# Reordering an attention loop: the third batch's output projection between the last two turns of maxima, and four small products at the loop's start

## The reference

```python
x = x + attention(layernorm(x))     # 16 heads of 16, softmax, with biases
x = x + ffn(layernorm(x))           # silu(x W1) * (x W3), Walsh-Hadamard, W2
x = x + memory(layernorm(x))        # gated values, decaying sum along the sequence, gate, Wo
x = x + ffn(layernorm(x))
# attention, for each head:
scores = Q @ K.T / sqrt(16);  attn = softmax(scores);  out = attn @ V
return concat(out) @ Wo.T + bo
```

## Time and profile before

| | |
|---|---|
| three runs | 562.08, 563.42 (median), 564.31 us |
| the profiled execution | 561.39 us, of which 559.6 us is the span from the first to the last instruction |
| TensorE busy in the records | 547.4 us |
| VectorE, ScalarE, GpSimd busy | 385.8, 311.7, 192.6 us |
| the attention loop | from about 34.9 to 242.7 us of the span |

### The profile page before, as it was taken

One profiled execution on the slowest core, in us unless ns is written; L12 is line 12 of the kernel. 1 busy time (PEld: TensorE's weight loads), 2 busy tenths in 40 slices (PEclk: granted clock), 3 DMA queues, 4 the chain that ended last, 5 costly groups with the idle time before them and its releaser, 6 DMA issues.

```text
span 559.6 us, 8472 instructions
## 1 busy us (share of the span) xinstructions
PE 547.4 (98%) x2932; PEld 368.2 (66%) x2932; DVE 385.8 (69%) x727; ACT 311.7 (56%) x581; POOL 192.6 (34%) x221
## 2 busy tenths in 40 slices
PE   8999999999999998999999999999999999999997
PEld 5553343344435433468888888888888888888887
DVE  6898988898898899836475555756886437364433
ACT  3668889876987787753333233366775323323231
POOL 4795367562546252520122012422332012102120
PEclk9999999999999999999999999999999999999999
DMA  7465440230023030021122221210000202223121
GB/s 218 109 197 168 141 134 3 72 127 32 3 97 132 2 152 4 2 75 21 19 43 33 34 42 18 43 18 1 0 2 0 34 12 43 64 39 76 25 52 39
DMA packets 74554, 32.54 MB, mean 58 GB/s; under 512 B 59608, under 2 KB 67800, under 8 KB 74128
## 3 DMA queue, kind: packets, MB, share of 16 engines
q1 hardware_dynamic: 73292, 30.93, 20.6%
q10 hardware_dynamic: 1220, 1.07, 0.6%
HBM read 10.89 MB, written 5.24 MB: 29 GB/s over the span
## 4 chain that ended last, share of the span: by engine, by line
PE 87%; DVE 5%; ACT 3%; issue 2%; SPq 2%; DMA 1%; ACTq 0%; POOL 0%; DVEq 0%
PE PS L426 85%; DVE mxr L1141 2%; SPq L384 2%; PE PS L437 1%; ACT PR L966 1%; DMA xf<-PR 1%; PE PS L624 1%; DMA ring<-mT 1%; ACT AOh L838 0%; DVE PR L1280 0%; DVE OT L1206 0%; ACT PR L1034 0%; ACT XNs L1028 0%; ACTq L928 0%; DVE X L1315 0%
## 5 line engine op out<-in xcount | busy, mean ns | idle before, releaser
L426 PE MATMUL PS<-xTh,ring 128*128 128x512 f32 x608 | 187.5, 391 | 0.0
L1141 DVE TENSOR_REDUCE mxr<-PS 128x1 f32<-128x512 f32 x256 | 162.9, 681 | 24.0 <-PE PS L426 23.1
L966 ACT ACTIVATE PR<-PS 128x512 f32<-128x512 f32 x256 | 138.0, 602 | 29.8 <-PE PS L426 29.3
L426 PEld LDWEIGHTS PS<-xTh,ring 128*128 128x128 f32 x608 | 113.4, 188 | 24.5 <-issue 1.7
L426 PE MATMUL PS<-xTl,ring 128*128 128x512 f32 x304 | 109.8, 390 | 0.0
L838 ACT ACTIVATE AOh<-PR 128x512 fp32r<-128x512 f32 x72 | 45.5, 632 | 112.0 <-DVE PR L1280 106.5
L426 PE MATMUL PS<-ring 48*128 48x512 f32 (+1 forms) x512 | 99.4, 451 | 4.5 <-DVE mxr L1141 2.8
L1280 DVE TENSOR_TENSOR PR<-PR,PS 128x512 f32<-128x512 f32 x64 | 43.5, 679 | 66.2 <-PE PS L426 45.5
L426 PEld LDWEIGHTS PS<-ring 50*128 50x128 f32 (+1 forms) x512 | 41.4, 185 | 71.0 <-ACT PR L966 43.5
L1402 POOL TENSOR_TENSOR xTl<-xf,xTh 128x512 fp32r<-128x512 f32 x30 | 41.9, 1410 | 134.1 <-ACT xTh L838 134.1
L1133 DVE TENSOR_TENSOR AOl<-PR,AOh 128x512 fp32r<-128x512 f32 x72 | 55.2, 767 | 45.5 <-ACT AOh L838 45.4
(11 more groups left out here) (142 smaller groups left out, 728.8 us busy)
## 6 DMA issues: line engine op xcount, KB each, us to landing
ring<-qh SPq DMA_DIRECT2D x48, 128.0 KB, 2.8
xf<-PR SPq DMA_DIRECT2D x112, 32.0 KB, 1.9
ring<-ql SPq DMA_DIRECT2D x24, 128.0 KB, 2.8
ring<-weight_scratch SPq DMA_DIRECT2D x3, 1024.0 KB, 4.8
Vp<-qf SPq DMA_DIRECT2D x96, 32.0 KB, 1.9
weight_scratch<-in_w SPq DMA_DIRECT2D x2, 1024.0 KB, 6.7
X<-in_x SPq DMA_DIRECT2D x3, 512.0 KB, 4.8
out<-X SPq DMA_DIRECT2D x6, 256.0 KB, 2.4
```

Source lines behind the costliest of these rows:

```text
L426: return nc.tensor.matmul(dst, lhsT, rhs, start=start, stop=stop, skip_group_check=True)
L966: nc.scalar.activation(PR[:, j % 8, :], PS[:, kq_bank(j), :], ACT.Exp, scale=HD ** -0.5)\
L1141: nc.vector.tensor_reduce(mxr[:, S % 2, blk, TT * p + t:TT * p + t + 1], PS[:, QK0 + i % 3, :], AX.X, ALU.max, negate=True).then_inc(max_d ...
```

## The change

Four things are edited.

1. In steps 1 and 2 of the loop TensorE makes a product of ones with 192 columns behind each half's scores, into a bank that nobody reads; four in all.
2. In the middle batches the second halves trade places: values at s = 24, 26 and the output projection at s = 28, 30 (before the other way round), with the waits of the shared bank changed to suit. The last batch has a table of its own: the projection of the third batch at s = 12, 14 and 16, 18 (before s = 20 whole, then 24 and 26), and the last turn of maxima at s = 20 (before s = 19).
3. ScalarE makes the high part of a batch's first `AOf` at s = 31 (last batch: s = 21; before s = 28 in all). GpSimd makes its low part at s = 6 of the next batch (last batch: s = 22; before s = 29), and the low part of the second at s = 7 (before s = 6).
4. In the last batch VectorE's split of the second weight goes to s = 26 to 29 (before 23 to 26).

```diff
-OUT_AT = ((20,), (24, 26))
-V_AT = ((22,), (28, 30))
-
-MAX_AT = 3
+OUT_AT = ((20,), (28, 30))
+V_AT = ((22,), (24, 26))
+
+LAST_OUT_AT = ((12, 14), (16, 18))
+
+MAX_AT, LAST_MAX_AT = 3, 20
+
+AO_AT, LAST_AO_AT = STEPS - 1, 21
...
+        def out_at(b):
+            return LAST_OUT_AT if b == BATCH - 1 else OUT_AT
+
+        def turned_at(K):
+
+            S = (K + LEAD) // 8 - 1
+            if S == LAST_GROUP - 1:
+                return S if K % STEPS == LAST_MAX_AT else None
+            return S if K % 8 == MAX_AT and S < LAST_GROUP else None
...
-                elif s // 8 < 3 and b < BATCH - 1:
+                elif b == BATCH - 1:
+
+                    pe.wait_ge(x_done, 2 * b - 2 + 2 * (s == LAST_MAX_AT))
+                elif s // 8 < 3:
                     pe.wait_ge(qk_f, 4 * b + 2 * (s // 8))
-                elif s // 8 == 3:
-                    pe.wait_ge(*((x_done, 2 * b) if b else (w2h_done, 3)))
+                else:
+                    pe.wait_ge(*((v_copied, 2 * b + 4) if b else (w2h_done, 3)))
...
-                    pe.wait_ge(*((v_copied, 2 * b + 2) if b > 1 else (w2h_done, 4)))
+                    pe.wait_ge(*((x_done, 2 * b - 2) if b > 1 else (w2h_done, 4)))
...
+                for half in range(2):
+                    at = out_at(b)[half]
+                    if b and s in at:
+                        if s == at[0]:
+                            pe.wait_ge(aol_done, 2 * b)
+                            pe.wait_ge(mt_ready, turned)
+                            if half and not more:
+                                pe.wait_ge(x_done, 2 * b - 1)
+                        for part in range(2) if len(at) == 1 else (at.index(s),):
+                            out_projection(half, part)
...
+                    if K in (1, 2):
+
+                        keep_busy(1, OB, FILL // 2)
...
-                if s == OUT_AT[1][-1] + 2:
+                if s == (LAST_AO_AT if b == BATCH - 1 else AO_AT):
                     act.wait_ge(aof_ready, 2 * b + 1)
...
-                            if s == OUT_AT[half][-1] + 1:
+                            if s == out_at(b)[half][-1] + 1:
                                 add_attention(b - 1, half)
...
+                    for w, at in ((W_UP, SPLIT_AT), (W_LIN, 26)):
+                        if at <= s < at + 4:
+                            w_split_hi(w, s - at)
...
                 if s == 6 and b:
+                    output_lo(2 * b - 1)
+                if s == 7 and b:
                     output_lo(2 * b)
-                if s == OUT_AT[1][-1] + 3:
+                if s == LAST_AO_AT + 1 and b == BATCH - 1:
                     output_lo(2 * b + 1)
```

More of the change, by code:

```diff
@@ L365, in _ @@
                         weights_in(W_LIN)
[L366 to L369, removed]
+                    S = turned_at(STEPS * b + s)
+                    if S is not None:
+                        max_rows(S)
                     if b == 0 and s == 24:
@@ L677, in shared_bank @@
                     if s == V_AT[1][0]:
-                        pe.wait_ge(mt_ready, turned)
+                        pe.wait_ge(v_copied, 2 * b + 3)
                     project_v(b + 1, 1, V_AT[1].index(s))
@@ L693, in _ @@
                     weigh_values((K - 3) // 2)
-                S = (K + LEAD) // 8 - 1
-                if s % 8 == MAX_AT and S < LAST_GROUP:
+                S = turned_at(K)
+                if S is not None:
                     turn_maxima(S, b, s)
@@ L1007, in _ @@
                             qk_split(b + 1, n)
-                if s % 8 == MAX_AT and (K + LEAD) // 8 - 1 < LAST_GROUP:
-                    max_evacuate((K + LEAD) // 8 - 1)
+                S = turned_at(K)
+                if S is not None:
+                    max_evacuate(S)
             act.wait_ge(aof_ready, 2 * BATCH)
@@ L1264, in _ @@
                     moments(TT * ((b + 2) % BATCH), TT, b + 3)
-                if b == BATCH - 1 and SPLIT_AT <= s < SPLIT_AT + 8:
-                    w_split_hi((s - SPLIT_AT) // 4, (s - SPLIT_AT) % 4)
+                if b == BATCH - 1:
+                    for w, at in ((W_UP, SPLIT_AT), (W_LIN, 26)):
+                        if at <= s < at + 4:
+                            w_split_hi(w, s - at)
             S = LAST_GROUP - 1
```

## The result

The changed kernel takes 574.46 us (median of four runs, 571.93 to 574.66) against 562.75 us: ratio 1.021, 95% interval 1.017 to 1.024. Slower, as forecast, but by 11.7 us and not by 5.7: the time lies above the range. The profiled execution took 574.44 us, span 572.6. The kernel before does not always run alike: of 60 further runs of it 35 have a mean granted clock of 0.999 or 1.00, all at 560.4 to 561.6 us, and 25 one of 0.981 to 0.997, up to 570 us. The first thing in the changed kernel's profile that differs from before is the mean granted clock of TensorE, 0.984 for 1.00.

The account below looks back on a forecast made before the run. TensorE was taken to set the pace in the middle batches, VectorE in the last, ScalarE behind the last turn. The terms 0.0 - 0.5 + 7.3 - 1.1 = +5.7 us gave 569.1 us from 563.42, range 567 to 571 (8 in 10: 565.6 to 571.5).

Parts of the forecast that it names:

- The term that was to decide: At s = 4 of batches two to four VectorE waits 2.7 us for GpSimd's low part of `AOf`; +7.3 us.
- The clock rival: TensorE's clock falls behind the three waits, a pair of steps taking twice as long: +9.7 us, 578.8; chance 0.03.
- the ones at 0.0: Four products of ones in steps 1 and 2 fill TensorE's idle time: 0.0 us, upper bound 1.3.
- The traded halves: Middle batches: TensorE no longer waits for VectorE's add before the turn at s = 27; -0.5 us.
- Last batch to step 116: Steps 108 to 115 get a projection part in each pair, so step 116 starts 1.1 us later.
- Its end: Last batch behind step 116, paced by ScalarE's exponentials; whole last-batch term -1.1 us, bounds -1.4 and 0.
- the rival with the late maxima: The tail wins nothing, maxima's DMAs need 4.3 us, second batch loses 2.7: 570.4, up to 571.5 us; chance 0.07.

Follow-up runs that it names:

- e1: Changed kernel with the low part of the first `AOf` moved from s = 6 to s = 0 of the next batch: 559.87 us, ratio 0.996.
- e4: Kernel before with only the low part of the first `AOf` moved to s = 6 of the next batch: 579.25 us, ratio 1.031.
- e11: Changed kernel plus eight products with a zero tile on TensorE between the halves of steps 38, 70 and 102: 567.85 us.
- e6: Kernel before with the four products of ones alone added: 562.11 us, all eleven runs at clock 1.00.
- e5: Changed kernel with the first `AOf`'s low part at s = 0 and without the four products of ones: 559.87 us.
- e12: Changed kernel with middle batches and low parts as before, leaving the products of ones and the last batch's changes: 560.03 us, ratio 0.995.
- e8: Changed kernel with the low part of the first `AOf` at s = 4, ahead of the two placings of values: 565.37 us.
- e3: Changed kernel without the four products of ones: 576.34 us, runs from 571.25 to 582.48.

## Why the prediction was wrong

*Direction and mechanism were right.* The term that was to decide did: the low part of `AOf` behind the placings, three waits of VectorE (forecast 2.7 each; 2.96, 2.60, 2.58), three of TensorE at the very products named, +7.8 for +7.3. e1 shows it by removal, e4 by itself.

*The step that failed: "products behind each wait could run at half speed; no row here shows a lower clock, so the sum goes without it".* The clock rival had 3 in 100, and was priced at 9.7 us. It happened in addition to the waits, for 5.9 us by the landmarks and 7 by e11. That before showed a full clock was evidence only for a TensorE that in the loop never waits longer than 0.81 us; the change made waits about three times as long (2.18 to 2.54). The Trainium skill, "TensorE: Matmul & The Clock Gate", Part 1, has the idle array fall to 1.2 GHz, and by the rows behind each wait the trace of the changed kernel agrees (0.50); the rule had been weighed and left out for want of a row. My sum would have been 569.1 + 9.7 = 578.8 with the rival's price and 575 with the measured one. Without the clock's part the forecast was near: e11, at full clock, is 6.4 us above before (567.4 for 561.0), the ones' 1.1 included, against +5.7.

*The second step that failed: the ones at 0.0.* I named an upper bound of 1.3 and took the other end, by a wait of 0.18 us before the last scores of step 3. The idle time there was larger than that wait, 0.9 us, but 2.1 us of products do not fit into it. That the cost lies just under the bound is luck: the bound had a third of a microsecond for each product and no cover, where each took 0.52 and 0.9 in all was covered. e6 measures 1.1, e5 against e1 1.1. And "the clock is already full, so there is nothing to win" was read from one execution; 25 of 60 runs of before are below 0.999, and of the 33 runs of e1, e6 and e12 none is.

*What held.* The traded halves: -0.5 forecast, -0.6 in the trace with the crossings, 0.2 in the runs. Last batch to step 116: +1.1, as forecast to a tenth. Its end: the term was -1.1 net, measured -1.7 (e12: -2.1), since exponentials come at 0.49 and the late maxima cost TensorE 0.54 us but ScalarE nothing; a size, 0.3 beyond its bound of -1.4.

With both failed terms at their measured sizes the sum is 5.7 + 5.9 + 1.2 = 12.8 of the 13.0 us between the two profiled executions. That it comes so near is partly luck, since the other differences (+0.8 before the loop, +0.5 in the waits, -0.1, -0.6 and -0.4) nearly cancel. Two of its sums are a little off and decide nothing: ScalarE's work behind the last turn adds up to 13.0 and not 12.9, and the upper end of the rival with the late maxima to 571.7 and not 571.5.

## What to carry to other kernels

When an operation is moved down an engine's list, ask first who overwrites what it reads, and where that writer stands: one low part moved behind two placings of values made three waits of 2.6 to 3.0 us, though GpSimd was busy only a third of the time. Price a wait on TensorE at its length plus what the lower clock costs behind it, here three quarters as much again (5.9 for 7.8), also when the trace of before shows a full clock throughout. And look at the clock of all runs, not of the profiled one, before calling a keep-busy product useless.

## What was not expected of the hardware

- An idle time of 1.18 us on TensorE, with shorter waits around it, was followed by a stretch at 0.50 (e8); 1.02 and 0.81 us in the middle batches were not, in the same execution, and neither was one of 2.18 us in e3. What decides between them I did not settle.
- The same waits of 2.6 us were followed by low stretches of some 3, 3 and 10 us in the changed kernel and of 7, 7 and 20 us in e4. In both cases the products ran back to back or nearly so in these stretches. Why it lasted longer stays open.
- A float32 product with 128 columns took 0.24 us from start to start in a row of its kind (28 records in 3.39 us for 14 products), and a short product of another kind between scores has a fixed part of about 0.26 us beside its columns (0.39 at 96, 0.52 at 192).
